# Every matmul but the transposes as four of 32 output rows, in four column groups of the array

## The reference

```python
x = x + attn(layernorm(x))          # q, k, v = xn @ Wq, xn @ Wk, xn @ Wv; 16 heads of 16
# scores = q k^T, causal; softmax(scores / 16); ctx = attn @ v; ctx @ Wo + bo
x = x + ffn(layernorm(x))
# xd = mx_quantize(xn), wd = mx_quantize(W); out = xd @ wd.T + bias
```

## Time and profile before

| | us |
|---|---|
| median of 3 runs | 2092.31 (2090.9 to 2093.17) |
| the profiled execution | 2085.36, span of its instructions 2083.6 |

### The profile page before, as it was taken

One profiled execution on the slowest core, in us unless ns is written; L12 is line 12 of the kernel. 1 busy time (PEld: TensorE's weight loads), 2 busy tenths in 40 slices (PEclk: granted clock), 3 DMA queues, 4 the chain that ended last, 5 costly groups with the idle time before them and its releaser, 6 DMA issues.

```text
span 2083.6 us, 35416 instructions
## 1 busy us (share of the span) xinstructions
PE 1980.0 (95%) x11749; PEld 755.4 (36%) x11749; DVE 1716.6 (82%) x4358; ACT 1351.9 (65%) x2881; POOL 810.7 (39%) x1123
## 2 busy tenths in 40 slices
PE   6799899999999999999999999999999999999984
PEld 3333333333333343434334343433333433333433
DVE  4797886869887978796897879797889899888875
ACT  5357566767766767676766666666766666677661
POOL 3323414231335554553243646453345444211232
PEclk9999999999999999999999999999999999999997
DMA  4442221414041241703323161340614121130000
GB/s 155 123 111 64 77 68 38 102 48 120 9 123 55 74 99 38 174 11 81 93 53 95 46 140 50 79 102 17 160 39 112 54 55 40 39 90 24 9 31 21
DMA packets 162963, 152.04 MB, mean 73 GB/s; under 512 B 32982, under 2 KB 150492, under 8 KB 162780
## 3 DMA queue, kind: packets, MB, share of 16 engines
q1 hardware_dynamic: 162780, 149.77, 27.0%
HBM read 91.89 MB, written 57.02 MB: 71 GB/s over the span
## 4 chain that ended last, share of the span: by engine, by line
PE 71%; DVE 19%; ACT 3%; issue 3%; POOL 2%; SPq 2%; DMA 1%; POOLq 0%; ACTq 0%; DVEq 0%
PE psum L1496 20%; PE psum L1479 19%; PE psum L1464 16%; DVE max_parts L1201 8%; PE psum L1560 8%; PE psum L1553 5%; DVE psum L1196 4%; ACT probs L1005 2%; SPq L674 1%; PE psum L1531 1%; DVE max_parts L1196 1%; ACT acc_sb L1014 1%; PE psum L1582 1%; PE psum L1523 1%; DVE stats L1259 1%
## 5 line engine op out<-in xcount | busy, mean ns | idle before, releaser
L1005 ACT ACTIVATE probs<-psum 128x512 f32<-128x512 f32 (+3 forms) x2560 | 1211.6, 536 | 518.9 <-PE psum L1479 511.8
L1201 DVE TENSOR_REDUCE max_parts<-psum 128x1 f32<-128x512 f32 x1536 | 965.2, 682 | 123.6 <-PE psum L1464 119.5
L1479 PE MATMUL psum<-q_rows,k_rows 99*128 99x512 bf16 (+3 forms) x2560 | 856.1, 351 | 3.3 <-ACT probs L1005 1.9
L1464 PE MATMUL psum<-k_rows,q_rows 96*128 96x512 bf16 (+3 forms) x2560 | 815.7, 349 | 30.2 <-DVE max_parts L1201 11.4
L1496 PE MATMUL psum<-probs,v_in 128*17 128x512 f32 (+3 forms) x5120 | 594.3, 536 | 11.9 <-ACT acc_sb L1014 11.5
L1196 DVE CUSTOM_DVE_ANT_0 psum<-psum,causal 128x128 f32<-128x128 f32 (+3 forms) x1024 | 476.5, 518 | 135.5 <-PE psum L1464 132.7
L1479 PEld LDWEIGHTS psum<-q_rows,k_rows 99*128 99x128 bf16 x2560 | 237.2, 97 | 640.5 <-ACT probs L1005 500.3
L833 POOL TENSOR_SCALAR_AFFINE_SELECT probs<-probs 128x512 f32<-128x512 f32 x256 | 165.9, 648 | 727.3 <-ACT probs L1005 727.1
L1464 PEld LDWEIGHTS psum<-k_rows,q_rows 96*128 96x128 bf16 x2560 | 244.6, 98 | 291.7 <-DVE max_parts L1201 81.8
L1496 PEld LDWEIGHTS psum<-probs,v_in 128*17 128x17 f32 x5120 | 86.1, 95 | 226.7 <-issue 162.1
L1196 DVE DVE_READ_ACCUMULATOR2_ANT max_parts<- 128x1 f32 x1024 | 144.9, 141 | 0.0
(11 more groups left out here) (161 smaller groups left out, 1268.7 us busy)
## 6 DMA issues: line engine op xcount, KB each, us to landing
q_rows<-qk_scratch SPq DMA_DIRECT2D x384, 64.0 KB, 2.7
k_rows<-qk_scratch SPq DMA_DIRECT2D x384, 64.0 KB, 2.7
qk_scratch<-shop SPq DMA_DIRECT2D x56, 384.0 KB, 3.2
sums_scratch<-acc_sb SPq DMA_DIRECT2D x48, 256.0 KB, 2.3
shop<-in_L_attn_x SPq DMA_DIRECT2D x19, 512.0 KB, 5.2
v_scratch<-shop SPq DMA_DIRECT2D x16, 544.0 KB, 4.3
v_in<-v_scratch SPq DMA_DIRECT2D x64, 136.0 KB, 2.6
out_shop<-in_L_attn_x SPq DMA_DIRECT2D x12, 512.0 KB, 8.5
```

The costliest lines, as they stand in the source:

```text
L1005: nc.scalar.activation(probs[s % NPROBS][:, h, a:CHUNK], bank[SCORE_BANKS[n % 3]][:, a:CHUNK], ACT.Exp, scale=SCALE).then_inc(probs_ready, 1)
L1201: nc.vector.tensor_reduce(max_parts[k % 2][:, first:first + heads, t % TILES, c], ring_bank(UNIT_USE[n])[:, 0:heads * width] .rearrange("p ...
L1464: ins = nc.tensor.matmul(dst[:, i * width:(i + 1) * width], q_rows[u][0:ROWS, qc, first + i, t % TILES * P:(t % TILES + 1) * P], k_rows[u] ...
L1479: nc.tensor.matmul(bank[SCORE_BANKS[n % 3]][:, a:CHUNK], k_rows[u][0:ROWS + LEVELS, h, kb * P:(kb + 1) * P], q_rows[u][0:ROWS + LEVELS, qc ...
```

## The change

A helper cuts the output rows of a matmul into four of 32 (COLUMNS) and issues four matmuls in place of one, with a quarter of the weight columns each and the same moving operand. `scores`, `unit`, `project`, `linear` and `bias` call it; `values` already has a head in each column group, and the transposes stay. The semaphore increment is on the last of the four. Semaphores, slots, banks and the other engines are unchanged.

```diff
+COLUMNS = 32
...
+            def by_columns(out, weights, moving, start, stop):
+
+                for r in range(0, P, COLUMNS):
+                    ins = nc.tensor.matmul(out[r:r + COLUMNS], weights[:, r:r + COLUMNS], moving, start=start, stop=stop)
+                return ins
...
-                    ins = nc.tensor.matmul(dst[:, i * width:(i + 1) * width],
-                                           q_rows[u][0:ROWS, qc, first + i, t % TILES * P:(t % TILES + 1) * P],
-                                           k_rows[u][0:ROWS, first + i, c * CHUNK:c * CHUNK + width],
-                                           start=True, stop=True)
+                    ins = by_columns(dst[:, i * width:(i + 1) * width],
+                                     q_rows[u][0:ROWS, qc, first + i, t % TILES * P:(t % TILES + 1) * P],
+                                     k_rows[u][0:ROWS, first + i, c * CHUNK:c * CHUNK + width], True, True)
...
-                nc.tensor.matmul(bank[SCORE_BANKS[n % 3]][:, a:CHUNK],
-                                 k_rows[u][0:ROWS + LEVELS, h, kb * P:(kb + 1) * P],
-                                 q_rows[u][0:ROWS + LEVELS, qc, h, a:CHUNK],
-                                 start=True, stop=True).then_inc(scores_ready, 1)
+                by_columns(bank[SCORE_BANKS[n % 3]][:, a:CHUNK], k_rows[u][0:ROWS + LEVELS, h, kb * P:(kb + 1) * P],
+                           q_rows[u][0:ROWS + LEVELS, qc, h, a:CHUNK], True, True).then_inc(scores_ready, 1)
...
-                    ins = nc.tensor.matmul(ring_bank(use), w[:, e, (m % 2) * P:(m % 2 + 1) * P], xnT[n % 2][:, e, :],
-                                           start=e == 0, stop=e == EH - 1)
+                    ins = by_columns(ring_bank(use), w[:, e, (m % 2) * P:(m % 2 + 1) * P], xnT[n % 2][:, e, :],
+                                     e == 0, e == EH - 1)
...
-                        ins = nc.tensor.matmul(ring_bank(use)[:, j * E:(j + 1) * E], xT[:, e, t * P:(t + 1) * P],
-                                               w[:, e, :], start=start and e == 0,
-                                               stop=e == EH - 1 and (start or j == 1))
+                        ins = by_columns(ring_bank(use)[:, j * E:(j + 1) * E], xT[:, e, t * P:(t + 1) * P], w[:, e, :],
+                                         start and e == 0, e == EH - 1 and (start or j == 1))
...
-                nc.tensor.matmul(ring_bank(use), onesb[:, :], bias_rows[i][:, None, :].broadcast_to([P, 2, E]),
-                                 start=True, stop=False)
+                by_columns(ring_bank(use), onesb[:, :], bias_rows[i][:, None, :].broadcast_to([P, 2, E]), True, False)
```

## The result

The changed kernel takes 2038.2 us, the kernel before beside it 2092.7: a ratio of 0.974, with a 95% interval of 0.9725 to 0.9759, or 55 us less. The prediction was 2031.

The account below looks back on a forecast made before the run. PE's own pace was taken to bound the kernel. Edges give 91 us, DVE takes back 30, so 61 less: 2092.3 becomes 2031. Its own range was 1993 to 2085; for eight in ten it reached up to 2490.

Parts of the forecast that it names:

- The price of 0.205 us: On PE, time lost at the two edges of every values block, where the tile shape changes.
- Removed and added edges: On PE: edges go at 640 values blocks, 62 pairs come round transposes; 91 us less.
- all 578 pairs: Net pairs of edges fewer on PE: 640 removed less 62 added.
- The single factor of 77%: Share of values blocks on the path, 421 of 544 us, applied to all 578 pairs of edges, giving 445.
- Groups at no cost: On PE, a group of four matmuls takes the array as long as one did, with loads covered: 0 us.
- The third rival: Column-group loads on PE not covered by matmuls: 28 ns per group, 134 us, 2165 us at most; chance 0.12.
- the fourth: The four matmuls on PE don't run side by side: over 5 ms; chance 0.02.
- Given back: PE stalls for DVE where DVE is nearly full: 30 us of the gain lost, with ends of 10 and 60.
- The front end: PE can't be fed 30.4 thousand pairs of load and matmul fast enough: 2490 us; chance 0.27.
- DVE taking it all: PE's gain only turns into waits for the ring: 2075 to 2092 us; chance 0.08.
- The price of 80 ns a pair: Front end's assumed time on PE per load and matmul: 2432 us, plus 55 for start and tail.

Follow-up runs that it names:

- scores_only: The changed kernel with only the scores in column groups, units and all items with 128 output rows: 2344.2 us, 1.120 of the kernel before.
- two_of_64: The changed kernel with its matmuls cut into two groups of 64 output rows instead of four of 32: 2104.7 us, 1.005 of the kernel before.
- the moves: The load of x issued four slots earlier, the denominators' inversion on DVE three slots later; in the kernel before: 2096.9 us (1.0034).
- slack_after: The changed kernel with the load of x issued four slots earlier and the denominators' inversion on DVE three slots later: 2022.5 us (0.9682).
- quarters: The changed kernel with the moving columns of each score and unit cut in four, 91.8 thousand pairs in all: 2909.9 us (1.392).
- halves: The changed kernel with the moving columns of each score and unit cut in two, 50.9 thousand pairs in all: 2078.1 us (0.9934).

## Why the prediction was right, point by point

**What bounds.** Right: PE did. The price of 0.205 us for the two edges of a values block was read from start-to-start times in the earlier trace rows, and the cause, the tile's shape and not the type, from the earlier trace rows. `scores_only` (0.12 and 0.10 between bf16 products) shows both, and `two_of_64` (no gain) that cutting alone does nothing. Too narrow was that the column counts must be equal: 48 columns beside 64 have no edge. It doesn't touch the count of the change itself, where 48 meets 32.

**Removed and added edges.** The term was 91 us. With the DVE work and SP's late loads both out of the way the gain is 99 us (107 with the moves' own cost) of the 118 that all 578 pairs would give. So the term was near, and 8 us or more too low. The single factor of 77% was too simple: edges round items were on the path for all of their price (28 us measured for 130 pairs), and those of `turn_max` for a quarter to a little over half (3 and 7 of 12 us).

**Groups at no cost.** Right for time on the array: 0.22 us for a group, with its loads covered. The third rival (loads not covered) is refuted by the timeline after, and the fourth with it. PE's loads are 828 us busy after, against 755, beside the matmuls; one of 32 bf16 columns takes 96 to 97 ns, where one of 128 took 97 to 98. The rule of the Trainium skill ("TensorEngine Tiling (Array Packing)", Restrictions) that column tiling excludes the fast load may hold all the same; no run here shows a cost of it.

**Given back.** The prediction had -30 for DVE, with ends of 10 and 60. Of the 99 us, 99 - 55 = 44 were given back: 18 to DVE's maxima (73 against 55), 16 to the late transfers (`slack_after`; 12.5 by the ratios, 20 by the pair with the moved plan in both), and about 10 that show only when both are gone. The term was short by a third, and it had the wrong composition: it put all on DVE's own work, and SP was named nowhere. The queue's own rows, with loads 0.47 us apart and twelve of them for each of the 64 pairs k, weren't read. The error was partly covered by the first term, which was low as well (91 for 99).

**The sum.** 61 forecast, 55 measured. Both terms were too small, by 8 and by 14 us, and the sum is nearer than either reason for it: that is partly luck.

**The rivals.** The front end (0.27) didn't decide, but it is no phantom: `quarters` comes to 31 ns a pair, the change asks for one in 54 in a dense stretch, and at one in 27 (`halves`) the kernel is already slower by 40 us, though the supply isn't shown to be all of that. The price of 80 ns a pair, taken between 57 and 153, was far too high for every execution but the one of 3814.4 us (75 ns), of which no trace tells the cause. Of the two figures of the Trainium skill ("TensorE: Matmul & The Clock Gate", Wait — 56ns, not 53.3ns?), 62 ns per matmul from microcode is refuted for this setting: `quarters` gets a load and a matmul through in 31. The other, a floor of 25 ns from start to start, doesn't hold across column groups: 32 pairs take 14 ns each in its burst. DVE taking it all (0.08) didn't happen; its share of the chain rose from 19% to 27% as foretold, and its busy share is 84%, with 85% expected.

## What to carry to other kernels

Read PE's timeline from start to start and price each neighbouring pair: where a matmul with another tile size follows (32, 64 or 128 output rows, with 17 under 32 and 48 under 64), some 0.1 us is lost on each side, and a kernel with one small column-tiled product in every step pays it twice per step. Bringing the large products into the same tile shape costs nothing on the array as long as the groups come no faster than the front end supplies them, and it pays to bring the small items along, since a whole item between grouped ones pays both edges. Once PE is faster, look at the queue that issues its loads at its own pace, and give their consumers more distance in the plan: here that was worth another 12 to 16 us, while the same moves cost the kernel before 8.

## What of the hardware was not expected

- PE's instructions come in bursts of 14 ns a pair, but over the whole of `quarters` one pair came in 31 ns, with 630 us of waits that the trace can't name. Twice the changed kernel's density of scores and units cost 40 us (`halves`), 14 of them in such waits.
- A transpose of 48 columns has no edge beside groups of 64, and the scores behind it start 0.01 us later (`two_of_64`); beside groups of 32 or whole tiles it has both edges.
- Both gaps of 5.5 us on PE were followed by a stretch at the lower clock: 0.83 and 0.86 granted in the 20 us round them, 0.50 right behind them, 1.00 in the same work without the gap. These stalls cost more than their length.
- Four column groups may stream the same moving operand at full rate; a group of four 512-column matmuls takes 0.22 us, as one with 128 output rows does.
